# The experts' second layer as three fp32r passes over high and low parts, two groups behind the first layer

## The reference

```python
logits = x2 @ Wr + br
expert = jnp.argmax(probs, axis=-1)
...
buf = jnp.zeros((e * CAP, d), x2.dtype).at[slot].add(xd)
h = jax.nn.gelu(jnp.einsum('ecd,edf->ecf', buf, W1) + b1[:, None, :], approximate=False)
out = jnp.einsum('ecf,efd->ecd', h, W2) + b2[:, None, :]
y = out.reshape(e * CAP, d)[slot]
return y * (gate * keep.astype(x2.dtype))[:, None]
```

## Time and profile before

| | |
|---|---|
| time before, median of 3 runs | 1586.62 us (1584.03 to 1586.75) |
| the profiled execution | 1587.35 us |
| its span in the trace | 1585.6 us |
| mean granted TensorE clock | 0.977 of full speed |
| PE busy | 1496.5 us (94%), 11213 records |
| DVE, ACT, POOL busy | 1085.5, 1156.2 and 1023.7 us |
| first product of `experts` | 1098.3 us after the start |
| first product of the second layer's group 0 | 1103.19 us |
| second layer of groups 78 and 79 starts | 1370.61 us |

### The profile page before, as it was taken

How to read it: one execution, slowest core, us unless ns; L and a number is a source line. 1 busy time by engine, 2 the same in 40 slices (tenths; PEclk the granted TensorE clock), 3 DMA queues, 4 the chain that set the end, 5 groups by cost and what they waited for, 6 DMA issues and landing times. The chain is left out here.

```text
span 1585.6 us, 33983 instructions
## 1 busy us (share of the span) xinstructions
PE 1496.5 (94%) x11213; PEld 1381.3 (87%) x11213; DVE 1085.5 (68%) x2864; ACT 1156.2 (73%) x3447; POOL 1023.7 (65%) x1068
## 2 busy tenths in 40 slices
PE   5549999999999999999999999987999999699999
PEld 2248999999999999999999999977999999699999
DVE  6757787787887887877878787752333333288887
ACT  5539888888888888888888888854555555355554
POOL 5856557878878878878788787663756655422221
PEclk9869999999999999999999999998999999899999
DMA  6323221221211111100000000002334334244444
GB/s 233 131 92 115 96 70 52 69 68 48 59 57 46 56 55 50 46 27 15 14 14 15 15 15 7 4 5 52 83 99 101 84 74 116 64 140 129 131 128 114
DMA packets 157790, 110.59 MB, mean 70 GB/s; under 512 B 28115, under 2 KB 145341, under 8 KB 157616
## 3 DMA queue, kind: packets, MB, share of 16 engines
q1 hardware_dynamic: 140208, 88.25, 18.6%
q0 software_dynamic: 17408, 20.16, 4.6%
HBM read 54.23 MB, written 70.17 MB: 78 GB/s over the span
## 5 line engine op out<-in xcount | busy, mean ns | idle before, releaser
L918 ACT ACTIVATE expd<-masked,nmax 128x128 f32<-128x128 f32 x1024 | 396.0, 393 | 0.0
L729 POOL TENSOR_TENSOR prob<-expd,rtotal 128x1024 f32<-128x1024 f32 x128 | 243.0, 1898 | 143.8 <-DVE rtotal L996 142.9
L1013 DVE COPY_PREDICATED masked<-off_diag,ps_s 128x1024 f32<-128x1024 int32 x128 | 174.9, 1366 | 149.4 <-PE ps_s L816 149.4
L858 PE MATMUL ps_o<-u,probT 128*128 128x128 f32 x2048 | 249.2, 275 | 0.7 <-issue 0.7
L858 PEld LDWEIGHTS ps_o<-u,probT 128*128 128x128 f32 x2048 | 239.1, 192 | 0.9 <-issue 0.9
L918 ACT ACTIVATION_READ_ACCUMULATOR expd<-masked,nmax 128x1 f32 x1024 | 197.0, 192 | 0.0
L927 ACT ACTIVATE u<-ps_ut 128x1024 f32<-128x1024 f32 x128 | 131.4, 1027 | 67.8 <-PE ps_ut L869 67.8
L1028 DVE TENSOR_TENSOR w_lo<-ps_w,w_hi 128x512 fp32r<-128x512 f32 x256 | 164.4, 681 | 5.8 <-ACT w_hi L948 5.8
L941 ACT ACTIVATE probT<-ps_ut 128x1024 f32<-128x1024 f32 x128 | 131.5, 1028 | 45.0 <-PE ps_ut L824 38.3
L948 ACT ACTIVATE w_hi<-ps_w 128x512 fp32r<-128x512 f32 x256 | 146.5, 596 | 19.4 <-PE ps_w L846 12.7
L1019 DVE TENSOR_REDUCE nmax<-masked 128x8 f32<-128x1024 f32 x128 | 155.5, 1214 | 2.5
(11 more groups left out here) (228 smaller groups left out, 4074.9 us busy)
## 6 DMA issues: line engine op xcount, KB each, us to landing
answers_sp<-zeros SPq DMA_DIRECT2D x16, 512.0 KB
answers_fq<-zeros SPq DMA_DIRECT2D x16, 512.0 KB
sh_back<-answers_sp SPq DMA_DIRECT2D x56, 128.0 KB, 2.4
sh_back<-answers_fq SPq DMA_DIRECT2D x56, 128.0 KB, 2.4
out<-res SPq DMA_DIRECT2D x56, 128.0 KB, 1.9
h_sb<-in_L_tok_weight SPq DMA_DIRECT2D x12, 512.0 KB, 5.4
table<-h_sb SPq DMA_DIRECT2D x12, 512.0 KB
sent_sp<-zeros SPq DMA_DIRECT2D x8, 660.0 KB, 3.0
```

The source lines that it names most:

```text
L729: nc.gpsimd.tensor_tensor(prob[k % 2][:, :].rearrange("p (g j) -> p g j", g=H), expd[k % 2][:, :].rearrange("p (g j) -> p g j", g=H), rtot ...
L858: mm = nc.tensor.matmul(ps_o[:, 0:D], probT[k % 2][:, g * N:(g + 1) * N], u[k % 2][:, g * D:(g + 1) * D], start=(g == 0), stop=(g == H - 1))
L918: ins = nc.scalar.activation(expd[(k - 1) % 2][:, g * N:(g + 1) * N], masked[(k - 1) % 2][:, g * N:(g + 1) * N], ACT.Exp, bias=nmax[(k - 1 ...
L1013: nc.vector.copy_predicated(masked[k % 2][:, :].rearrange("p (g j) -> p g j", g=H), off_diag[:, :].unsqueeze(1).to_broadcast([P, H, N]), p ...
```

## The change

The second layer's operands are split, as the first layer's are. The GELU values `hid` get a rounded fp32r copy `hid_hi` and a remainder `hid_lo`; the weights `w2` get `w2_hi` and `w2_lo`. The product is then three fp32r products for each half and block (high x high, high x low, low x high) in place of one plain float32 product. The second layer runs two groups behind the first one instead of one, so each engine's loop has a step more. The rounding is divided: ACT copies blocks 0 to 2 of `hid` in one instruction of 768 columns, POOL copies block 3 (256 columns) as soon as its GELU, now the first of the four, is there. DVE forms `hid_lo` in two subtractions (256 and 768 columns), splits `w2` in the first step of an expert (two instructions of 512 columns), and copies the token numbers behind `xT_lo` instead of ahead of it; the split of the first-layer weights moves a step later. ACT's copy and POOL's wait until the second layer of two groups ago is done. SP waits for the new `tokens` and `w2_lo` counts.

```diff
+        hid_hi = [sb(f"hid_hi{k}", [P, FC, G], F32R) for k in range(2)]
+        hid_lo = [sb(f"hid_lo{k}", [P, FC, G], F32R) for k in range(2)]
+        w2_hi = [sb(f"w2_hi{k}", [P, FC, D], F32R) for k in range(2)]
+        w2_lo = [sb(f"w2_lo{k}", [P, FC, D], F32R) for k in range(2)]
...
-        S = {n: sem(n) for n in ("turned", "xhi", "xlo", "up", "gelu", "down", "out", "late")}
+        S = {n: sem(n) for n in ("turned", "xhi", "xlo", "up", "gelu3", "gelu", "hid3", "hidhi", "hidlo", "down", "out", "late", "tokens", "w2_hi", "w2_lo")}
...
-            for t in range(-4, ALL + 2):
+            for t in range(-4, ALL + 3):
...
+                    need(sp, S["w2_lo"], expert(i, a) - 1)
...
-                    need(sp, S["xlo"], group(i, a) - RING + 1)
+                    need(sp, S["tokens"], group(i, a) - RING + 1)
...
-                if live(i, k - 1):
-                    c, w = (k - 1) % 2, side(k - 1)
-                    need(pe, S["gelu"], group(i, k))
-                    need(pe, S["out"], group(i, k) - 2)
+                if live(i, k - 2):
+                    c, w = k % 2, side(k - 2)
+                    need(pe, S["hidlo"], group(i, k) - 1)
+                    need(pe, S["w2_lo"], expert(i, k - 2) + 1)
+                    need(pe, S["out"], group(i, k) - 3)
                     for b in range(2):
+                        o, at = ps_o[c][:, b * D:(b + 1) * D], slice(b * P, (b + 1) * P)
                         for f in range(FC):
-                            mm = nc.tensor.matmul(ps_o[c][:, b * D:(b + 1) * D], hid[c][:, f, b * P:(b + 1) * P],
-                                                  slot[w].w2[:, f, :], start=(f == 0), stop=(f == FC - 1))
+                            hi, lo = hid_hi[c][:, f, at], hid_lo[c][:, f, at]
+                            nc.tensor.matmul(o, hi, w2_hi[w][:, f, :], start=(f == 0), stop=False)
+                            nc.tensor.matmul(o, hi, w2_lo[w][:, f, :], start=False, stop=False)
+                            mm = nc.tensor.matmul(o, lo, w2_hi[w][:, f, :], start=False, stop=(f == FC - 1))
...
+                    need(act, S["hidlo"], group(i, k) - 1)
+                    for f in (FC - 1, *range(FC - 1)):
+                        ins = nc.scalar.activation(hid[c][:, f, :], ps_h[c][:, f, :], ACT.Gelu, bias=slot[side(k)].b1_c[:, f:f + 1])
+                        if f == FC - 1:
+                            ins.then_inc(S["gelu3"], 1)
+                    ins.then_inc(S["gelu"], 1)
+                    need(act, S["gelu"], group(i, k) + 1)
                     need(act, S["down"], group(i, k) - 1)
-                    for f in range(FC):
-                        ins = nc.scalar.activation(hid[c][:, f, :], ps_h[c][:, f, :], ACT.Gelu, bias=slot[side(k)].b1_c[:, f:f + 1])
-                    ins.then_inc(S["gelu"], 1)
+                    nc.scalar.activation(hid_hi[c][:, 0:FC - 1, :], hid[c][:, 0:FC - 1, :], ACT.Copy).then_inc(S["hidhi"], 1)
...
-                a = k + 2
+                a = k + 1
                 if opening(i, a):
                     dve.wait_ge(s_w[side(a)], loads(i, a))
                     need(dve, S["up"], group(i, a) - EACH)
                     split_expert(nc, dve, slot[side(a)], S["w_hi"], S["w_lo"], expert(i, a) + 1)
+                if live(i, k) and k % EACH == 0:
+                    need(dve, S["down"], group(i, k) - EACH)
+                    w = side(k)
+                    nc.vector.tensor_copy(w2_hi[w][:, :, :], slot[w].w2[:, :, :]).then_inc(S["w2_hi"], 1)
+                    dve.wait_ge(S["w2_hi"], expert(i, k) + 1)
+                    nc.vector.tensor_tensor(w2_lo[w][:, :, :], slot[w].w2[:, :, :], w2_hi[w][:, :, :].bitcast(F32),
+                                            ALU.subtract).then_inc(S["w2_lo"], 1)
+
+                if live(i, k - 1):
+                    c = (k - 1) % 2
+                    need(dve, S["hid3"], group(i, k))
+                    nc.vector.tensor_tensor(hid_lo[c][:, FC - 1, :], hid[c][:, FC - 1, :], hid_hi[c][:, FC - 1, :].bitcast(F32), ALU.subtract)
+                    need(dve, S["hidhi"], group(i, k))
+                    nc.vector.tensor_tensor(hid_lo[c][:, 0:FC - 1, :], hid[c][:, 0:FC - 1, :], hid_hi[c][:, 0:FC - 1, :].bitcast(F32),
+                                            ALU.subtract).then_inc(S["hidlo"], 1)
 
                 if live(i, k + 1):
                     c, r = (k + 1) % 2, (k + 1) % RING
                     need(dve, S["xhi"], group(i, k) + 2)
                     need(dve, s_scattered[r], ring(i, k + 1) * 32)
-                    nc.vector.tensor_copy(tokens[r][:, :], rows[r][:, :, D])
                     nc.vector.tensor_tensor(xT_lo[c][:, :], ps_x[c][:, 0:G], xT_hi[c][:, :].bitcast(F32), ALU.subtract).then_inc(S["xlo"], 1)
-
-                if live(i, k - 1):
-                    c, r = (k - 1) % 2, (k - 1) % RING
-                    need(dve, S["down"], group(i, k))
-                    plus = slot[side(k - 1)].b2_b[:, :].unsqueeze(1).to_broadcast([P, 2, D])
+                    nc.vector.tensor_copy(tokens[r][:, :], rows[r][:, :, D]).then_inc(S["tokens"], 1)
...
+                if live(i, k - 2):
+                    c, r = k % 2, (k - 2) % RING
+                    need(dve, S["down"], group(i, k) - 1)
+                    plus = slot[side(k - 2)].b2_b[:, :].unsqueeze(1).to_broadcast([P, 2, D])
...
-                if live(i, k - 1):
-                    r, b = (k - 1) % RING, bank_of(i, k - 1, bank)
-                    need_apart(pool, S["out"], group(i, k))
+                if live(i, k):
+                    c = k % 2
+                    need(pool, S["gelu3"], group(i, k) + 1)
+                    need(pool, S["down"], group(i, k) - 1)
+                    nc.gpsimd.tensor_copy(hid_hi[c][:, FC - 1, :], hid[c][:, FC - 1, :]).then_inc(S["hid3"], 1)
+                if live(i, k - 2):
+                    r, b = (k - 2) % RING, bank_of(i, k - 2, bank)
+                    need_apart(pool, S["out"], group(i, k) - 1)
                     for half in range(2):
                         nc.gpsimd.indirect_dma_start(
```

## The result

The changed kernel takes **1659.89 us**, median of 4 runs (1655.35 to 1662.06), beside 1586.41 for the kernel before in the same comparison (1584.03 to 1586.75). The ratio is 1.0463, with a 95% interval of 1.0439 to 1.0487: **slower by 4.6%**. Its profiled execution took 1659.77 us, 72.4 more than that of before (1587.35).

What follows compares the result with a forecast made beforehand. The prediction took PE, a gapless queue of matmuls in the experts stage, to bound the kernel: 1587.35 + 73 (second layer) + 2.5 (start) - 0.6 (end) = 1662.3, so 1662 us, range of this case 1656 to 1675.

Steps and rivals of the forecast that it cites:

- The load of the stationary operand sets the price: Second layer on PE: each narrow fp32r product costs its own weight load, 0.112 us, not its streamed columns.
- 24 x 0.112 = 2.69 us, step 4.34: PE's second layer: 24 products take 2.69 us a group for 1.78, so a step goes from 3.43 to 4.34 us.
- upper bound: Price of one new second-layer product on PE: at most 0.118 us, that of the fp32r product with 256 columns.
- the +73: PE's longer second layer: +0.91 us a group over 80 groups, in all +73 us.
- Other engines fit under 4.34: Expert steps: ACT about 3.0 us, DVE 2.6 to 3.7, POOL at most 3.3 (4.6 with a late tile, lag held).
- POOL's sum: POOL per group: scatters 2.56 us plus the new copy, at most 3.3 us, 4.6 in 16 late-tile steps.
- Start +2.5, end -0.6: Stage's start: PE stands still about 2.5 us for xT_lo; stage's end: POOL's smaller scatter backlog saves 0.6 us.
- SP: nothing: SP's queue: new waits and weights waiting one step later cost nothing; row loads keep the same two steps.
- Rival 1, columns: Second-layer products priced by columns, 0.059 us: about 1575, chance 0.08; about 1597 if POOL takes the gain, 0.03.
- Rival 2, float32's rate: Narrow fp32r products in the second layer cost 0.222 us each: +284 us, about 1871; chance 0.09.
- Rival 3, a new wait: Chain of ACT copy and DVE subtractions makes xT_lo late for PE: at 0.3 us a step about 1685; chance 0.11.
- the 1.3 us of slack: Copy chain on ACT and DVE up to xT_lo: 3.2 us against 4.5 until PE wants it, 1.3 us spare.

Runs made afterwards that it cites:

- half_columns: The changed kernel with each of the 24 second-layer products streaming 64 columns instead of 128, half the outputs not computed; ratio 1.0429 to the kernel before.
- wide: The changed kernel with operands exchanged: w2's parts stationary, GELU parts streaming 256 columns, 12 products, result left transposed; ratio 1.0015 to the kernel before.
- two_passes: The changed kernel without the product of low GELU part and high weights, 16 products instead of 24; ratio 1.0135 to the kernel before.
- bf16_ring: The changed kernel with bf16 parts, POOL's copy on DVE, eight ring buffers, xT_lo first on DVE, scatter wait moved to the token copy; ratio 1.0001.
- plain_ring: plain_act_copies with eight ring buffers instead of five, xT_lo first in DVE's step, scatter wait moved to the token copy; ratio 1.0107 to the kernel before.
- bf16_ring_late_weights: bf16_ring with SP asking for the weights three steps later, behind the rows of three more groups; 1569.21 us, ratio 0.9898 to the kernel before.
- plain_act_copies: plain_float32 with ACT rounding all four blocks and no copy on POOL; ratio 1.0124 to the kernel before.
- bf16_act_copies: The changed kernel with the four part tiles in bf16 and ACT copying all four blocks, none on POOL; ratio 1.0173 to the kernel before.
- plain_float32: The changed kernel's schedule, second layer back as float32 products of the high parts, low parts made but not used; ratio 1.0111 to the kernel before.

## Why the prediction was right

It said 1662 (own range 1656 to 1675), and 1659.89 was measured. Its steps in order:

- **The load of the stationary operand sets the price.** Right, and shown from three sides: half_columns (half the columns, same time), wide (half the loads, 1.44 us for 2.62), two_passes (16 loads, the old step). The router's product with 16 columns was the row that carried it.
- **24 x 0.112 = 2.69 us, step 4.34.** Measured 2.62 and 4.31: the term was mis-sized by a little. (The reason that the prediction gives for its upper bound is worded the wrong way round: what makes 0.118 a bound is that a product with 128 columns can't be dearer than one with 256.) Twenty-three starts are 0.111 apart, but the first product follows one of 256 columns, behind which its load fits, and costs 0.06. Of the +73 this took back 80 x 0.07 = 5.6. Transposes and first layer took 1.68 a step (1202.62 - 1200.94) where they had 3.43 - 1.78 = 1.65, which gives 2.4 back, and a few longer steps (4.55, 4.74, 5.52, where before had one of 4.61) some 0.7: 70.5.
- **Other engines fit under 4.34.** Right in the result. ACT's copy was put at 0.81 and took 0.85, DVE's subtractions at 0.42 and 0.96 and took that, POOL's copy at up to 0.73 and took 0.42. POOL's sum went wrong elsewhere: a scatter takes 1.15 us in the stage where it took 0.99, and the gap between copy and first scatter is 0.7. It stayed covered.
- **Start +2.5, end -0.6.** Measured +1.5 and -0.35 (the last scatter starts at 1450.57, 2.8 us after the last second layer, in place of 3.15). The start was mis-sized twice: the chain from the last GELU to `xT_lo` takes 2.2 us and not 2.7, and PE has its transposes to do meanwhile. PE, ACT and DVE there:

```profile
1104.39 0.38 PE L1293 MATMUL ex_ps_x<-ident,ex_rows 128*128 128x128 f32 x2
1106.31 0.39 PE L1303 MATMUL ex_ps_h<-ex_xT_hi,w_hi 128*128 128x256 f32 x1 [1.53 <-DVE ex_xT_lo L1375]
```

```profile
1104.08 0.84 ACT L1343 ACTIVATE ex_hid_hi<-ex_hid 128x768 fp32r<-128x768 f32 x1
1104.83 0.36 ACT L1331 ACTIVATE ex_xT_hi<-ex_ps_x 128x256 fp32r<-128x256 f32 x1
```

```profile
1104.96 0.96 DVE L1368 TENSOR_TENSOR ex_hid_lo<-ex_hid,ex_hid_hi 128x768 fp32r<-128x768 f32 x1 [1.07 <-ACT ex_hid_hi L1343]
1105.83 0.42 DVE L1375 TENSOR_TENSOR ex_xT_lo<-ex_ps_x,ex_xT_hi 128x256 fp32r<-128x256 f32 x1
```

  The copy starts 0.03 after the GELUs' end (1102.48 + 1.57 = 1104.05), not 0.3, and two operations start before the one ahead of them has ended: `xT_hi` at 1104.83, the copy's end being 1104.92, and `xT_lo` at 1105.83, the long subtraction's end being 1105.92. `xT_lo` ends at 1106.25 and ends PE's wait, as said. The stage itself began 1.2 us later, which no step of the prediction had, and the two errors nearly cancel: that is luck.
- **SP: nothing.** Right for this kernel and wrong as a reading. The added lag on the weights' wait was seen (two steps, 6.9 to 8.7 us), but only its effect on the split of the weights was weighed. The row loads queued behind it were given "the same two steps" before and after. By the program they had three before (10.3 us) and have two after (8.6 at a step of 4.3). In bf16_ring and plain_ring, once an expert, PE gets the rows 6.8 to 8.3 us after that second layer (1204.52 to 1212.83 is one case; the change of bank is left out), where two steps are 6.0 and 6.8: so at a step of 4.3 they are in time with little to spare, at 3.4 or 3.0 they are late, and moving the wait repairs it (bf16_ring_late_weights).
- **Rival 1, columns.** Out. Its second half, though, that something else takes the gain away once PE's step is short, is what wide showed: 1.44 us of second layer and a ratio of 1.0015. It named POOL's copy; plain_act_copies and bf16_act_copies have no copy on POOL and lose as much. The traces name a wait for scatters, SP's order, and at the change of bank POOL's backlog, so POOL was half right; the price of each is not shown apart, but for SP's order with bf16 parts (1.0%).
- **Rival 2, float32's rate.** Out: 0.111, not 0.222.
- **Rival 3, a new wait.** It did not come: `xT_lo` is late for PE three times, 2.7 us in all, 1.5 of it at the stage's start. The 21.5 us of DVE waits are for scatters, which the rival's chain doesn't hold, and PE's own time hides them. Whether the chain of copies has the 1.3 us of slack that the prediction gave it wasn't tried by lengthening it.

The Trainium skill, page "TensorE: Matmul & The Clock Gate", section "LDWEIGHTS (loading the stationary operand)", gives a load as its columns divided by 1.2 GHz, for 128 columns an estimated 107 ns. The trace agrees within 4%: 111 ns between starts. Its section "Weight-path perf modes — Fast Weight Load (FWL) and DoubleRow" says that the fast load is on for operands other than FP32 and brings nothing for fp32; with fp32r parts every product behind the first stayed at 111 ns and with bf16 parts it fell to 56, so the trace agrees there too, and fp32r loads as float32 does.

What stays open: what SP's order costs with float32 products (the late weights were only tried with bf16 parts; in plain_ring's trace 4.3 us of waits for rows and 8.2 us at the change of bank stand beside a time that is 1.1% or 17 us longer), and whether a smaller backlog on POOL would end the stall at the change of bank.

## What to carry to other kernels

Before trading one float32 product for three fp32r ones, count stationary loads, not passes: at 128 columns or fewer the load is the price, so the float32 product has two and the split has three, and the trade pays on PE only if the operand that streams is wide (256 columns here: 12 products in 1.44 us for 16 records in 1.78; the kernel as a whole gained nothing by it, 1.0015). Look for the row of a product with hardly any columns in the trace of before; it tells loads from columns without a run. And when the bound engine's work gets longer, the lags added elsewhere look free: put its old cost back into the new schedule once (as plain_float32 does) to see what they will cost as soon as anything makes it shorter.

## What the runs showed that wasn't expected

- The first narrow product behind a wide one is cheap: 0.06 us with 128 columns and 0.03 with 64, in place of 0.111.
- A scatter's issue on POOL takes longer beside DVE's subtractions. In the kernel after it takes 1.15 us on average in the stage against 0.99 before; the timeline of POOL has 0.98 and 1.16 side by side, and longer ones at the stage's end:

```profile
1202.34 1.16 POOL L1403 DMA_INDIRECT answers_sp<-res,tokens  x1 [0.71 <-DVE res L1382]
1203.80 0.98 POOL L1403 DMA_INDIRECT answers_sp<-res,tokens  x1 [0.30 <-issue]
...
1443.63 1.55 POOL L1403 DMA_INDIRECT answers_fq<-res,tokens  x1 [0.70 <-issue]
1445.49 0.97 POOL L1403 DMA_INDIRECT answers_fq<-res,tokens  x1 [0.30 <-issue]
```

  The long ones lie beside DVE's subtractions from SBUF in the timeline. In plain_ring, where DVE subtracts all 1024 columns in one operation of 1.22 us, scatters beside it take 1.82 (1197.86, with the subtraction from 1197.61) and the ones after it 0.98. No run isolated it.
- The granted clock can fall with PE busy. In half_columns it was 1.00 from 1124 to 1132 and 0.50 from 1136 to 1144, and PE had no gap from 1124 to 1148 (3.99 of 4.00 us in the window of the fall, all of the others). The other fall of that run came at a gap of PE of 0.82 us (1251.26 to 1252.08), with no gap in the 12 us ahead of 1248, and the clock stayed at 0.50 up to about 1271 with PE busy.
